# Layer 3 of a four-layer image model: one root for four units, by column tiles and row tiles

## The reference

```python
qkv = jax.nn.silu(x @ w_qkv.T)
q, k, v = jnp.split(qkv, 3, axis=-1)
q_flat = apply_rope(rms_norm(q.reshape(B, L, H, D), w_qn))
k_flat = apply_rope(rms_norm(k.reshape(B, L, H, D), w_kn))
...
scores = jnp.einsum('blhd,blwhd->blhw', q_flat, k_win) * scale
...
scores = scores - (1.0 - soft_mask) * 10000.0
attn = jax.nn.softmax(scores, axis=-1)
out = jnp.einsum('blhw,blwhd->blhd', attn, v_win).reshape(B, Hs, Ws, C)
out = rms_norm(out, w_on)
return jax.nn.silu((out + v) @ w_out.T)
```

## Time and profile before

| | |
|---|---|
| median of 3 runs | 3371.34 us (3361.9 to 3377.48) |
| the profiled execution | 3381.97 us, its span 3380.1 us |
| busy in the span | TensorE 89%, VectorE 63%, ScalarE 59%, GpSimd 34% |
| mean granted clock of TensorE | 0.946 of full speed |
| layer 3 | about the last quarter of the span; one image takes about 89 us in it |

### The profile page before, as it was taken

The page is one execution under the profiler, slowest core; times in us unless marked ns, Lnnn a source line. Parts: engine busy times, 40 slices in busy tenths (PEclk is TensorE's granted clock), DMA queues, the critical chain, the costliest instruction groups (busy, mean ns, idle before and its releaser), DMA issues. The chain is left out here.

```text
span 3380.1 us, 103119 instructions
## 1 busy us (share of the span) xinstructions
PE 3018.3 (89%) x43264; PEld 1668.5 (49%) x43264; DVE 2138.1 (63%) x5157; ACT 1995.5 (59%) x4348; POOL 1134.3 (34%) x1444
## 2 busy tenths in 40 slices
PE   6999999999985899999999977999995788888886
PEld 2333333333322565555565645667663555555553
DVE  5787778878753676767667643554553466665654
ACT  2667676766662556455556533555552677777774
POOL 3443433434311221222222201222221455554643
PEclk9999999999986999999999988999996899999997
DMA  6877778687763233333333214545444233333332
GB/s 200 163 170 153 172 171 179 143 187 162 145 142 114 62 86 81 73 89 86 86 69 81 67 47 148 159 150 169 149 148 145 69 92 115 117 115 113 117 103 76
DMA packets 299756, 414.89 MB, mean 123 GB/s; under 512 B 39424, under 2 KB 256288, under 8 KB 278304
## 3 DMA queue, kind: packets, MB, share of 16 engines
q1 hardware_dynamic: 275664, 272.46, 27.1%
q0 software_dynamic: 18432, 134.23, 19.9%
q10 hardware_dynamic: 5200, 1.62, 0.2%
HBM read 219.67 MB, written 53.81 MB: 81 GB/s over the span
## 5 line engine op out<-in xcount | busy, mean ns | idle before, releaser
L734 DVE TENSOR_TENSOR l_probs<-l_psum,l_decay 128x1024 f32<-128x1024 f32 x512 | 598.6, 1219 | 164.7 <-PE l_psum L630 154.0
L782 ACT ACTIVATE l_sizes<-l_probs 128x2048 f32<-128x2048 f32 x256 | 487.1, 1908 | 303.2 <-DVE l_probs L734 292.1
L1822 ACT ACTIVATE l_logits<-l_logits,l_low 128x100 f32<-128x100 f32 x1024 | 372.7, 366 | 203.4 <-DVE l_low L1802 202.7
L1829 POOL TENSOR_TENSOR l_logits<-l_logits,l_inv 128x400 f32<-128x400 f32 x256 | 242.9, 950 | 679.9 <-DVE l_inv L1808 679.2
L630 PE MATMUL l_psum<-l_qk 32*128 32x512 f32 x2048 | 340.2, 645 | 7.9 <-POOL l_qk L868 4.2
L883 POOL DMA_DIRECT2D l_sizes<-l_sizes x128 | 111.5, 871 | 549.3 <-ACT l_sizes L782 537.3
L1645 POOL TENSOR_TENSOR l_E<-l_E,l_causal 128x1024 f32<-128x1024 f32 x64 | 153.0, 2390 | 381.6 <-DVE l_x_act L1343 224.6
L645 PE MATMUL l_psum<-l_probs,l_V 128*32 128x512 f32 x2048 | 270.6, 600 | 1.7 <-DVE l_probs L734 1.6
L1814 DVE COPY l_PT<-l_psum 100x512 f32<-100x512 f32 x256 | 173.0, 676 | 114.4 <-PE l_psum L1774 113.9
L301 PE MATMUL l_psum<-l_xT,l_w_up 128*128 128x512 f32 x512 | 231.3, 606 | 9.1 <-DVE l_row_var L1401 9.0
L1789 PE MATMUL l_psum<-l_PT,l_V_windows 100*32 100x16 f32 x16384 | 202.6, 187 | 34.9 <-issue 22.6
(11 more groups left out here) (246 smaller groups left out, 5883.8 us busy)
## 6 DMA issues: line engine op xcount, KB each, us to landing
l_sizes<-l_sizes POOLq DMA_DIRECT2D x128, 1024.0 KB, 7.6
l_V_windows<-v_image SPq DMA_DIRECT2D x512, 100.0 KB
l_V_windows<-v_padded SPq DMA_DIRECT2D x512, 100.0 KB
l_E<-rows_c SPq DMA_DIRECT2D x64, 512.0 KB, 5.8
l_xT<-y SPq DMA_DIRECT2D x24, 1024.0 KB, 5.3
y<-l_res SPq DMA_DIRECT2D x32, 512.0 KB, 3.1
l_e_everywhere<-rows_e SPq DMA_DIRECT2D x112, 128.0 KB, 5.6
l_xT<-x SPq DMA_DIRECT2D x8, 1024.0 KB, 11.3
```

Of the source, the lines that this page charges most:

```text
L734: nc.vector.tensor_tensor(probs[:, N % 2, 2 * p:2 * p + 2, :], ring.region(name).rearrange("p (a n) -> p a n", a=2), decay[:, h:h + 2, s0: ...
L782: nc.scalar.activation(sizes[:, slot(N), :, :], probs[:, N % 2, :, :], ACT.Abs).then_inc(sized, 1)
L1822: nc.scalar.activation(e, e, ACT.Exp, scale=-1.0, bias=self.low[:, N % 4, i:i + 1], accum_out=self.total[:, N % 4, i:i + 1]).then_inc(self ...
L1829: nc.gpsimd.tensor_tensor(p, p, self.inv[:, N % 4, :].unsqueeze(2).to_broadcast([P, STEP, NKEY]), ALU.mult).then_inc(self.p_ready, 1)
```

## The change

The mean of a head is written once per head into 8 rows, not to all of its 32 channels: the matrix head_mean becomes 128 x 32, and four units fill one bank, each in a column tile of its own (32 partitions). ScalarE makes the root of the four at once (PACK = 4; two packs per image). A second matrix, head_spread, takes the root back to the channels: for each unit one matmul with 32 rows of the root, in the row tile in which they lie, into a bank of the ring. VectorE reads its factor from that bank and not from SBUF. Spreads are issued in pairs, both after both banks are free. The plan of steps changes (SQUARES_AT, PACK_AT, SPREAD_AT), the last pair is spread and scaled in step 3, there are four square buffers and two rec, and one more table is loaded.

```diff
+    c["head_mean_in_8"] = np.kron(np.eye(P // HD), np.full((HD, 8), 1.0 / HD)).astype(f)
+    c["head_spread"] = np.tile(np.kron(np.eye(P // HD), np.eye(8, 1) * np.ones((1, HD))), (4, 1)).astype(f)
...
-MEANS_AT = {12: (0, 2), 13: (2, 4), 14: (4, 6), 15: (6, 8)}
-ROOTS_AT = {12: (0, 2), 13: (2, 4), 14: (4, 6), 15: (6, 7)}
-SQUARES_AT = {10: (0, 2), 11: (2, 3), 12: (3, 4), 13: (4, 6), 14: (6, 8)}
-KEYS_AT = {14: (0, 1), 15: (1, 4)}
+PACK = 4
+PACK_AT = {12: 0, 14: 1}
+SQUARES_AT = {10: (0, 2), 11: (2, 4), 12: (4, 6), 13: (6, 8)}
+SPREAD_AT = {13: (0, 2), 14: (2, 4), 15: (4, 6)}
+LAST_SPREAD = 3
...
-                order += [("mean", b + 1, j) for j in range(*MEANS_AT.get(n, (0, 0)))]
+                order += [("rec", b + 1, j) for j in range(*SPREAD_AT.get(n, (0, 0)))]
+                order += [("mean", b + 1, PACK_AT[n])] if n in PACK_AT else []
+            if n == LAST_SPREAD and 0 < b < B:
+                order += [("rec", b, 6), ("rec", b, 7)]
             if n == 3 and b > 0:
                 order.append(("om", b - 1, 1))
...
+                def mean(b, m):
+                    name = ("mean", b, m)
+                    pe.wait_ge(sq_ready, 8 * b + PACK * (m + 1))
                     ring.may_fill(pe, name)
+                    for u in range(PACK):
+                        i = nc.tensor.matmul(ring.region(name)[32 * u:32 * u + 32, :], head_mean[:, :], square[:, u, :], start=True,
+                                             stop=True)
+                    i.then_inc(ring.filled(name), 1)
+
+                def spread(b, j0):
+                    pe.wait_ge(r_ready, 2 * b + j0 // PACK + 1)
+                    for j in (j0, j0 + 1):
+                        ring.may_fill(pe, ("rec", b, j))
+                    for j in (j0, j0 + 1):
+                        r = slice(32 * (j % PACK), 32 * (j % PACK) + 32)
+                        nc.tensor.matmul(ring.region(("rec", b, j)), head_spread[r, :], rec[r, j // PACK, :], start=True,
+                                         stop=True).then_inc(ring.filled(("rec", b, j)), 1)
...
-                for j in range(8):
-                    mean(0, j)
+                for m in range(2):
+                    mean(0, m)
+                    for j in range(PACK * m, PACK * (m + 1), 2):
+                        spread(0, j)
...
-                        if n % 8 == 0:
-                            pe.wait_ge(q_done, 4 * b + n // 4 + 2)
                         if n == 0:
-                            pe.wait_ge(k_done, 4 * (b + 1))
+                            for j in range(6):
+                                ring.is_taken(pe, ("rec", b, j))
+                        if n == 8:
+                            for j in (6, 7):
+                                ring.is_taken(pe, ("rec", b, j))
...
-                        for j in range(*MEANS_AT.get(n, (0, 0))):
-                            mean(b + 1, j)
+                        for j in range(*SPREAD_AT.get(n, (0, 0)), 2):
+                            spread(b + 1, j)
+                        if n in PACK_AT:
+                            mean(b + 1, PACK_AT[n])
+                    if n == LAST_SPREAD and 0 < b < B:
+                        spread(b, 6)
...
-                    nc.vector.scalar_tensor_tensor(k, k, w_qk[:, 0:1], rec[:, (u + 2) % 4, :].rearrange("p (r c) -> p r c", c=SIDE),
-                                                   ALU.mult, ALU.mult).then_inc(k_done, 1)
+                    nc.vector.scalar_tensor_tensor(k, k, w_qk[:, 0:1], ring.region(name).rearrange("p (r c) -> p r c", c=SIDE),
+                                                   ALU.mult, ALU.mult).then_inc(ring.took(name), 1)
...
-                    if n in (3, 4) and 0 < b < B:
-                        scale_query(b, 3 + n)
+                    if n == LAST_SPREAD and 0 < b < B:
+                        scale_query(b, 6)
+                        scale_query(b, 7)
...
+                    nc.scalar.activation(rec[:, m, :], ring.region(name), ACT.Ln, bias=eps4[:, :]).then_inc(ring.took(name), 1)
                     ring.is_taken(act, name)
+                    nc.scalar.activation(rec[:, m, :], rec[:, m, :], ACT.Exp, scale=-0.5).then_inc(r_ready, 1)
...
-                act.dma_start(head_mean[:, :], A["head_mean"]).then_inc(rest_loaded, 16)
+                act.dma_start(head_mean[:, :], A["head_mean_in_8"]).then_inc(rest_loaded, 16)
+                act.dma_start(head_spread[:, :], A["head_spread"]).then_inc(rest_loaded, 16)
                 act.dma_start(w.ident[:, :], A["ident"]).then_inc(rest_loaded, 16)
                 act.dma_start(w_on[:, :], A["L3_w_on"]).then_inc(rest_loaded, 16)
...
                     if b + 1 < B:
+                        if n in PACK_AT:
+                            root_of_mean(b + 1, PACK_AT[n])
                         for j in range(*SQUARES_AT.get(n, (0, 0))):
                             squares(b + 1, j)
```

More of the change, by code:

```diff
@@ L2199, in layer3_order @@
     order = [("gn", 0)] + [unit_name(u, -1) for n in range(4, 11) for u in layer3_units(n) if u[0] != "out"]
-    order += [("mean", 0, j) for j in range(8)]
+    for m in range(2):
+        order += [("mean", 0, m)] + [("rec", 0, j) for j in range(PACK * m, PACK * (m + 1))]
     for b in range(B + 1):
@@ L2243, in layer3 @@
         tanh = L.sb("tanh", [P, 2, BANK])
-        square = L.sb("square", [P, 3, BANK])
-        rec = L.sb("rec", [P, 4, BANK])
+        square = L.sb("square", [P, PACK, BANK])
+        rec = L.sb("rec", [P, 2, BANK])
         vs = L.sb("V", [P, NT, C])
@@ L2417, in _ @@
                             unit(unit_name(u, -1))
-                pe.wait_ge(rest_loaded, 176)
+                pe.wait_ge(rest_loaded, 192)
                 pe.wait_ge(consts_ready, 1)
-                for j in range(8):
-                    mean(0, j)
+                for m in range(2):
+                    mean(0, m)
+                    for j in range(PACK * m, PACK * (m + 1), 2):
+                        spread(0, j)
                 for N in range(B * STEPS + 10):
@@ L2463, in silu @@
                         if b > 0:
-                            ring.is_full(dve, ("mean", b - 1, 7))
+                            ring.is_full(dve, ("mean", b - 1, 1))
                         for e in range(2):
@@ L2526, in scale_query @@
                     half, g = u // 2, u % 2
-                    dve.wait_ge(r_ready, 8 * b + j + 1)
+                    name = ("rec", b, j)
+                    ring.is_full(dve, name)
                     if b > 0:
@@ L2588, in _ @@
                     if b + 1 < B:
[L2589 to L2592, removed]
-                    if n in (3, 4) and 0 < b < B:
-                        scale_query(b, 3 + n)
+                        for j in range(*SPREAD_AT.get(n, (0, 0))):
+                            if MEANS[j][0] == "k":
+                                scale_key(b + 1, number_of(j))
+                            else:
+                                scale_query(b + 1, j)
+                    if n == LAST_SPREAD and 0 < b < B:
+                        scale_query(b, 6)
+                        scale_query(b, 7)
                     if n in (5, 7) and b > 0:
@@ L2632, in squares @@
                         act.wait_ge(wp_ready, 2 * (b + 1))
-                    if at >= 3:
-                        ring.is_full(act, ("mean", (at - 3) // 8, (at - 3) % 8))
+                    if at >= PACK:
+                        ring.is_full(act, ("mean", (at - PACK) // 8, (at - PACK) % 8 // PACK))
                     ring.is_taken(act, (MEANS[j][0], b) + MEANS[j][1:])
-                    to = square[:, j % 3, :]
+                    to = square[:, j % PACK, :]
                     if MEANS[j][0] == "k":
@@ L2643, in squares, with root_of_mean @@
                         nc.scalar.activation(to, sq_q[:, number_of(j), :], ACT.Square).then_inc(sq_ready, 1)
[L2645 to L2647 removed]
+                def root_of_mean(b, m):
+                    name = ("mean", b, m)
                     ring.is_full(act, name)
[L2649 removed]
+                    if m == 0:
                         act.wait_ge(wp_loaded, 256 * (b + 1))
[L2651 to L2657, removed]
+                    if b > 0:
+                        ring.is_full(act, ("rec", b - 1, PACK * m + 3))
+                    nc.scalar.activation(rec[:, m, :], ring.region(name), ACT.Ln, bias=eps4[:, :]).then_inc(ring.took(name), 1)
                     ring.is_taken(act, name)
[L2659 removed]
+                    nc.scalar.activation(rec[:, m, :], rec[:, m, :], ACT.Exp, scale=-0.5).then_inc(r_ready, 1)
                 def copy_values(b, half, g):
@@ L2719, in _ @@
                 nc.scalar.preload_act_table_set("natural_log_exp_and_others")
-                for j in range(9):
-                    if j < 8:
+                for m in range(2):
+                    for j in range(PACK * m, PACK * (m + 1)):
                         squares(0, j)
-                    if j > 0:
-                        root_of_mean(0, j - 1)
```

(1 more changed line is left out.)

27 lines of the change are left out of this document (9 added, 18 removed).

## The result

The changed kernel takes 3418.39 us (median of 4 runs, 3402.87 to 3432.76) against 3374.41 us for the kernel before beside it: a ratio of 1.0131, 95% interval 1.0069 to 1.0193. That is slower by 1.3%, outside the range of 3357 to 3401. The profiled execution took 3402.87 us, the fastest of the four, with a span of 3401.0 us and a mean granted clock of 0.933 (0.946 before).

What follows compares the result with a forecast made beforehand. ScalarE was taken to set the pace of the stretch from step 10 into the next batch. Prologue 4.5, load 0.5, passages -3 and clock 7 summed to +9 us: median 3371.34 becomes 3380 us, range 3357 to 3401.

Steps and rivals of the forecast that it cites:

- The clock: TensorE in layer 3's passages: idle holes lower its clock, +1.0 us per passage (bounds 0 and 3.4), +7 in seven.
- two new holes: TensorE idle before each passage's two packs: 2.2 us before the first, 1.9 us before the second.
- the boundary's scores: Next batch's scores on TensorE wait for the keys' scalings: start 2917.7 instead of 2917.96, 0.3 us earlier.
- the mean waits for q6: Step 3: the output's mean needs q6's bank, waits 1.1 (spread) plus 1.3 us (scalings), starting 0.9 us later than before.
- the second rival: Clock falls in both holes of every passage and prologue stays at half clock: +30 us, 3401 us; chance 0.28.
- The prologue: Layer 3's units prepared with nothing beside them: +1.7 us at full clock, +8.1 at half; +4.5 taken.
- The waits: Chain through the ring's two banks in each passage: takes back ScalarE's 7.4 us relief, leaving -0.4 us per passage.
- the 1.2 us that the eighth root was to give back: Past the batch boundary, the eighth root no longer stands before the turned values: another 1.2 us earlier.
- the −3 of the prediction: Net of the passage replay at GpSimd's start: 0.9 - 1.32 = -0.4 us per passage, -3 us in seven.
- Scaling from PSUM: VectorE's scaling reading the spread root from PSUM: 685 ns against 746 from SBUF, pairs about 0.65 us each.
- q7's scaling: Step 4: the q7 scaling, 1.32 us on the chain, is gone because it is done in step 3.
- The extra load: One more table transfer on ScalarE's queue before the last one: bounds 0 and 0.64 us, +0.5 taken.

Runs made afterwards that it cites:

- e1_fill: Changed kernel plus matmuls whose result nobody reads in TensorE's four holes of each passage; ratio 1.0028 to the kernel before, passages 267.2 us.
- e7_fill_packs: Changed kernel with such unread matmuls only in the holes before the two packs of each passage; ratio 1.0075 to the kernel before.
- e2: e1_fill with unread matmuls also before the prologue's packs and spreads; ratio 1.0030 to the kernel before, prologue 31.69 us.
- e5: e2 without the fillers before the mean of the output, and the last pair spread in step 2; ratio 0.9968 to the kernel before.

## Why the prediction was wrong

**The clock, the step that failed.** The prediction took +1.0 us per passage, +7 in all, from bounds of 0 and 3.4, for "two new holes". There are four: it had foreseen that the boundary's scores wait for key 3 and that the mean waits for q6, and priced both as waits of other engines, but not as holes of TensorE (1.69 and 1.58 us). Measured between the changed kernel and e1_fill it is 24.3 us in seven passages, 3.5 each, above the upper bound, which was worked out for two (26.2 us with the stretches between). That is 0.9 us per hole where the prediction took 0.5: twice as many holes, and each dearer. The delays add up along the chain: in the passage shown, the second pack at half clock (1.93 for 1.05) makes ScalarE's root later, that the keys, and these the boundary's scores. The hole ahead of the scores does not grow by it: it is 1.69 us in all seven passages, and also in e7_fill_packs, whose packs run at the full clock. Taking a value near the low end, with "this stretch had 1.00 throughout" held against the second rival, was wrong: that 1.00 belongs to a stretch with eight means in it, which the change removes. (That it was these means that kept it up is argued, not shown; no run put them back alone.) It was also read from one batch: four of the seven passages had 0.91 to 0.95 before the change. The Trainium skill, "TensorE: Matmul & The Clock Gate", "Part 1: The HAM clock gate", says that an idle array goes to half rate and that activity releases it. The runs agree in kind, 0.78 with the holes and 0.97 with work in them, though TensorE was far from idle here: busy 229.40 of the 291.57 us.

**The prologue.** By the prediction's cut, first square to first row minimum, it takes 25.6 us (2635.46 to 2661.06), +8.0, against +4.5 taken and a bound of +8.1: all six TensorE pieces, packs and pairs of spreads, ran at half clock (1.93 to 2.08 us each). The sum of the steps was right: at the full clock 19.3 us was forecast, and e2 takes 19.87 (2633.16 to 2653.03).

**The waits, right in kind, one of them too cheap.** With the clock held, ScalarE's relief is indeed eaten by the ring: the boundary's scores in e2_fill_all begin 18.6 to 18.7 us after the table load in five of seven passages, 0.1 to 0.2 later than before (0.3 earlier was forecast), although ScalarE has 6.8 us less to do. The mean of the output is held by q6: at the full clock it starts 2.7 us after the spread (3098.82 to 3101.53 above), for 2.4 in the prediction, and spreading a step earlier shortened the passage by 2.2 to 2.7 us (e1 and e2 to e5). What did not come reliably is the 1.2 us that the eighth root was to give back, and which the prediction set against that price. In five passages of e2 the second turning of values starts about 21.4 to 22.0 us after the table load instead of 22.94; in the two others TensorE stops by itself in the weighing ahead of it (the row with 1.04 us of "issue" above) and starts at 22.6. The profile names no releaser for these stops, the kernel before has them too, and no run here took them away; their cause is open. So without the clock the passages came out at +2.1 us each (e1) where +0.9 was forecast, fillers included. With the stretches between them e1_fill is 2.8 us under the kernel before, close to the −3 of the prediction; that is partly luck, as the paragraph after the next shows.

**Scaling from PSUM.** Taken as 685 ns from another line; it is 743, for 746 from SBUF, so here the two sources cost the same. By the Trainium skill, "VectorE: DVE Perf Modes", section "The TRN2 errata — SBUF-src ops pay a fixed extra latency per instruction", it would have been, as an estimate from its cycles, some 65 ns more than from SBUF; the measured times differ from that. Four scalings take 2.72 us instead of 2.6, a few tenths per passage.

**What went better.** Between the passages 2.6 us came back on average, where only q7's scaling (1.32) was counted. One by one it is from −0.2 to 6.2: the stretches take 50.52 to 57.25 us before and 49.71 to 51.06 after. At a clock of 1.00 on both sides there are three each, 51.08 and 50.15 us on average, so 0.9 us came back. The rest lies in the other three of the kernel before (53.85, 57.25 and 54.47 us, clock 0.95 to 0.97), in which TensorE stops for 1.45 to 2.31 us without a releaser, as in the earlier trace rows; it can't be counted as a gain of the change. The extra load cost nothing that can be seen at its end: from the first issue on ScalarE's queue, ahead of the extra one (0.57 us), to the prologue's table load are 53.64 us, 53.86 before; from layer 3's first table load, behind the issues, 45.88 and 47.16.

**The sum.** In the trace: passages +39.1, prologue +7.7, the six stretches between −15.7, what is ahead of the prologue −1.3, between prologue and first passage −0.2, behind the last passage −2.7 (86.11 to 83.44): +27.0 us in layer 3 from its first table load on, against +9 forecast. The span grew by 20.9 us, since the layers before it happened to take 6 us less in that execution. The medians differ by 44 us with an interval of 23 to 65; the profiled execution is the fastest of the changed kernel, and the slower ones go with a lower clock (0.933 at 3402.87 and 3410.55 us, 0.930 at 3426.22, 0.926 at 3432.76), but where in them it fell no trace shows. The second rival, the clock falling in both holes and the prologue at half clock (3401 us, 0.28), was the case, with two holes too few.

## What to carry to other kernels

Before taking work away from TensorE, list every wait of the new plan in which it would stand idle, also those behind other engines' waits, and price the pieces right behind each of them at half clock. The gain on another engine can be outweighed so: here 6.8 us less ScalarE work per passage became 5.6 us more time in the passage, and useless matmuls in the holes gave 3.5 us of it back. A result that is spread through a short ring holds the ring until its reader is done; place it where nobody on the path needs the next bank (one step earlier was worth 2.2 to 2.7 us).

## What the hardware showed unexpectedly

A kernel got shorter by having TensorE busy longer: 229.40 us of its work in 291.57 us became 236.77 in 267.23. A scaling that reads one operand from PSUM took as long as the one from SBUF, 743 and 746 ns. Four matmuls of 512 columns in column tiles took 1.06 us and a pair in row tiles 1.13, where a mean of the kernel before took 1.12 alone on average.
